# Row maxima and inverse row sums turned in one step, the inverses spread by DMA

## The chip, the cores and the metric

The kernel runs on one core of one Trainium2 chip. The metric is the device time of one execution in microseconds (us), lower is better. Its engines are named as in the profile: PE (TensorE), with its weight loads as PEld, DVE (VectorE), ACT (ScalarE), POOL (GpSimd) and SP (SyncE), which here only issues DMAs.

## The reference

One layer over 4 batches of 512 tokens, width 512: causal cross attention to a context of width 128 (16 query heads of width 32 in 4 groups that share a key and value head), then a feed-forward part with a router.

```python
q = _rms_norm(_layernorm(x), q_norm_w); k = _rms_norm(ctx, k_norm_w)     # heads of 32, then rope on both
scores = jnp.einsum('bgnqd,bgkd->bgnqk', qg, k) * scale
scores = jnp.where(causal, scores, -1e30)
attn = jax.nn.softmax(scores, axis=-1)
out = jnp.einsum('bgnqk,bgkd->bgnqd', attn, v)                           # v is ctx, unnormalised
x = x + out @ w_out.T
# then, on t = _layernorm(x): softmax router, top 4 of 128, 8 basis units silu(t Wg) * (t Wu)
# mixed by the chosen experts' normalised amplitudes, a down product, and a shared pair of units
x = x + mixed_down + shared_down
```

All is in float32. The large products split each operand into a high and a low part (fp32r) and add three products.

## The kernel before

**Units of work.** Attention is cut into 32 spans: u = (batch, half of the queries, key head), so a span is 4 heads of 256 query rows. `TH` is 2 (tiles of 128 rows in a half), `G` is 4 (heads of a span). A span of the first half sees 256 keys, one of the second half 512. `KV` is 4, and u below 4 (the first half of the first batch) goes another way than the rest.

**First pass.** For each of the 8 blocks (head, 128 rows) of a span PE makes scores (`pass_a`, L1408), DVE adds the mask and takes the row's negated maximum (`row_max`, L1130), ACT takes the exponential with the row sum as a by-product (`row_sum`, L891). DVE inverts the 8 sums per row (`inverse`, L1147).

**Second pass.** It needs scores with keys as rows. For u < 4 PE turns the exponentials of the first pass (`turn_probabilities`, L1419), and ACT copies them from PSUM to `pr` (L907). For u from 4 on PE makes the scores again, turned (`pass_b`, L1432), with the maxima as two more contraction rows of `q_st` (high and low part, rows 96 and 97), so that ACT's exponential (L909) needs no bias; POOL zeroes the diagonal blocks (L797). Then PE multiplies by the values (`value_products`, L1445) into `o_bank`, and DVE multiplies by the inverse row sums, turned and repeated for the 32 rows of each head (`attended`, L1156, reading `r_t`).

**Maxima.** DVE splits them (`maxima_split`, L1139, L1141, `mhl`, 8 columns), PE turns the 8 columns (`maxima_turn`, L1388, one pair of transposes), ACT copies to `m_t` (L883), and two DMAs on SP put the rows into `q_st` (L617).

**Inverses.** POOL repeats each of the 4 columns 32 times (`spread_inverse`, L787, `rrep`), PE turns the 128 columns (`inverse_turn`, L1397, a pair), ACT copies to `r_t` (L898).

**Queries and keys.** Normalised and roped tiles (`rope`, on DVE for tiles in `ROPE_DVE`, else on POOL) are turned by PE (L1367; the first four, three-fold, at L1380), split on ACT and DVE, and stacked by 12 DMAs on SP for each span's queries (L609) and for each half's keys (L599). Tiles 0 and 5 are keys of the first batch, 1 to 4 the queries of u0 to u3, 6 to 9 those of u4 to u7.

**Order.** Every engine runs through the same numbered slots (-40 to 247), and in each slot does what is due there, in an order of its own that its loop spells out. `span_slot(u)` is where a span starts; `CORE` and `LEAD` (u < 4) give the slot offsets of its steps, `SPAN` the lengths (7 and 6 slots in the first batch; after it 4 for the first half, 8 or 9 for the second). From slot 32 on, the products of the projection (L1513), of the feed-forward units (L1529) and of the down step (L1550) fill the slots, two tiles of 128 tokens at a time from the slots in `START`; `PAIR_AT` and `TILE_AT` give the offsets of the router's steps. Slot 32 begins at about 75 us, and a slot takes over 3 us from there. Weights come by DMA (L572), ACT makes their high half (L856), DVE (L1186) and POOL (L814, one chunk of four) the low half.

**Banks.** Short products (scores, turns, router) take three PSUM banks in turn, in the order of `short_products`; each waits until the reader of the product three before is done.

Of the kernel before, what the change touches and what calls it, by code (L numbers as in the profile page):

```python
# [35 lines left out]
PAIR_AT = dict(choose=9, keep=9, coefficients=9, turn_choice=10, mix=12)  # L36
# [23 lines left out]
def attention_and_mixture_kernel(nc, x, ctx_in, q_norm_w, k_norm_w, w_out, w_router, w_units, w_down,  # L60
# [48 lines left out]
    with common:  # L109
# [19 lines left out]
        mx, sums, rinv = (sb(n, [P, 2, TH, G]) for n in ("mx", "sums", "rinv"))  # L129
        mhl, m_t = sb("mhl", [P, 2, TH, 2 * G], F32R), sb("m_t", [2 * G, Q], F32R)  # L130
        rrep, r_t = sb("rrep", [P, TH, P]), sb("r_t", [P, Q])
# [45 lines left out]
        def sem(name):  # L177
# [10 lines left out]
        s_m = [sem(f"m{i}_landed") for i in range(2)]  # L188
        s_chunk = [[sem(f"chunk{i}_{h}_landed") for h in range(2)] for i in range(WR)]
# [17 lines left out]
            "pass_a", "row_max", "row_sum", "max_high", "max_low", "max_turned", "max_out"))  # L207
        s_rinv, s_rrep, s_rt1, s_rout = (sem(n) for n in (
            "row_inverse", "inverse_spread", "inverse_turned", "inverse_out"))
        s_pb, s_ex, s_sel, s_pv = (sem(n) for n in ("pass_b", "exp", "exp_masked", "value_product"))  # L210
# [231 lines left out]

        def query_tile(u):
            return u // KV * NB + u % KV + 1
# [14 lines left out]

        def probable(u, k):  # L460

            first = span(u)[1] * TH
            if u < KV or k < first:
                return s_ex, step_no(u, k) + 1
            return s_sel, (u - KV) * TH + k - first + 1
# [47 lines left out]
        def short_products(s):  # L513
# [5 lines left out]
            if (u := of_span(s, "inverse_turn")) is not None:  # L519
                found.append(("inverse", u))  # L520
            if (u := of_later_span(s, "maxima")) is not None:
                found.append(("maxima", u - KV))
            for n in tiles_in(s, "turn"):
                found += stacks(n)
            found += [("scores", u * G * TH + m) for u, m in first_pass_tiles(s)[1:]]
            if (p := routing(s, "turn_choice")) is not None:
                found.append(("choice", p))
            if (g := mixture(s, "turn_x")) is not None:
                found.append(("x", g))
            if (g := turned_down(s)) is not None:  # L530
                found += [("down", 2 * g), ("down", 2 * g + 1)]
            if (p := routing(s, "mix")) is not None:
                found.append(("mix", p))
            return found
# [4 lines left out]
        short_read = dict(maxima=s_mout, turn=s_tl, inverse=s_rout, scores=s_max, x=s_txl, route=s_lg,  # L539
# [37 lines left out]
        def sync_engine(e):  # L577
# [34 lines left out]
            def rows(u):  # L612
                e.wait_ge(s_mout, u - KV + 1)
                if u >= QR:
                    e.wait_ge(*second_pass_over(u - QR))
                for k in range(2):
                    e.dma_start(f32(q_st[MAXROW + k:MAXROW + k + 1, u % QR, :, :]),  # L617
                                f32(m_t[k * G:(k + 1) * G, :])).then_inc(s_m[u % 2], 16)
# [24 lines left out]
            for s in slots:  # L643
                for b in range(2, B):
                    if s == batch_slot(b) + CONTEXT:
                        load_ctx(b)
# [8 lines left out]
                if s == LOADS[0]:  # L655
                    load_ctx(1)
                    load_x(1)
                if s == LOADS[1]:
                    load_x(2)
                if s == LOADS[2]:  # L660
                    first_weights()
                if (u := of_later_span(s, "maxima")) is not None:
                    rows(u)
# [3 lines left out]
                if (u := queries_stacked_in(s)) is not None:  # L667
                    stack_queries(u)
# [5 lines left out]
        def pool_engine(e):  # L674
# [108 lines left out]
            def spread_inverse(u):  # L783
                e.wait_ge(s_rinv, u + 1)
                if u >= 1:
                    e.wait_ge(s_rt1, u)
                e.tensor_copy(heads(rrep[:]), rinv[:, u % 2].unsqueeze(3).broadcast_to([P, TH, G, D])  # L787
                              ).then_inc(s_rrep, 1)

            def mask_probabilities(u, k):  # L790
# [5 lines left out]
                e.wait_ge(s_ex, n + 1)  # L796
# [27 lines left out]
            for s in slots:  # L824
                if (u := of_span(s, "spread")) is not None:
                    spread_inverse(u)
                if (step := second_pass_step(s - SELECT)) is not None:
                    mask_probabilities(*step)
                if (hb := of_half(s, "query_scale")) is not None:
                    query_scale(hb)  # L830
                if (g := mixture(s, "scales")) is not None:
                    norm_scale(g)
                if (hb := of_half(s, "key_scale")) is not None:
                    key_scale(hb)
                if (u := attended_before(s)) is not None:
                    out_low(u)
                for i, k in splits(s, "low"):
                    if k in POOL_LOW:
                        weights_low(i, k)
                for n in tiles_in(s - 1, "rope"):  # L840
                    if not rope_on_dve(n):
                        rope_last(n)
# [10 lines left out]
        def scalar_engine(e):  # L853
# [25 lines left out]
            def maxima_out(u):  # L879
                e.wait_ge(s_mt, u - KV + 1)  # L880
                if u > KV:
                    e.wait_ge(*max_rows(u - 1))
                e.activation(m_t[:], short("maxima", u - KV)[0:2 * G, 0:Q], ACT.Copy).then_inc(s_mout, 1)  # L883
# [10 lines left out]
            def inverse_out(u):  # L894
                e.wait_ge(s_rt1, u + 1)
                if u >= 1:
                    e.wait_ge(s_att, u)
                e.activation(r_t[:], short("inverse", u)[:, 0:Q], ACT.Copy).then_inc(s_rout, 1)  # L898

            def exponential(u, k):  # L900
                n = step_no(u, k)
# [74 lines left out]
            for s in slots:  # L976
                if (u := of_span(s, "inverse_turn")) is not None:
                    inverse_out(u)
                if (u := of_later_span(s, "maxima")) is not None:
                    maxima_out(u)  # L980
                if (u := attended_before(s)) is not None:
                    out_high(u)
                for n in tiles_in(s, "turn"):
                    high(n)
                if s - 1 in fillers and fillers[s - 1][0] == "unit":
                    tanh(fillers[s - 1])
                if (g := mixture(s, "turn_x")) is not None:
                    x_high(g)
                if (p := routing(s, "choose")) is not None:
                    router_exp(p)  # L990
                if (g := mixture(s, "normalize")) is not None:
                    normalize(g)
                if (g := mixture(s, "route")) is not None:
# [677 lines left out]
```

## Time and profile before

| | us |
|---|---|
| median of 3 runs | 856.6 |
| lowest and highest run | 853.35, 859.44 |
| the profiled execution, device time | 855.69 |
| its span, first to last instruction | 853.9 |
| PE, DVE, ACT, POOL busy in it | 786.6, 668.9, 577.1, 520.9 |

In the profile a row of a group gives the line, the engine, the operation, the tiles it writes and reads, the count, the busy time, the mean of one in ns, and the idle time of the engine just before such instructions with what ended it. Matmuls overlap in the pipeline, so the mean of one is longer than what one adds; the distance between starts tells that. A row of the timeline gives start and length in us. SPq is SP's issue of a DMA; its length is the issue, not the transfer.

### The profile page before, as it was taken

The page shows a single profiled execution, that of the slowest core. Times are in us where ns is not written, and L with a number is a line of the kernel's source. Part 1 is how long each engine was busy: PE and PEld are TensorE (multiplying, and loading weights), DVE is VectorE, ACT ScalarE, POOL GpSimd, SP SyncE. Part 2 cuts the span into 40 slices and gives each one's busy share as a digit, 9 for nine tenths or more (in the row PEclk, how much of TensorE's full clock was granted, in tenths as well). Part 3 has the DMA queues.
Part 4 walks back from the last instruction along what each step waited for, and adds up shares of the span by engine and source line. Part 5 has one row for each costly group of instructions (what it writes and reads, how often), then busy time and mean ns, then how long its engine had stood idle before and what let it go on. Part 6 is the DMA issues. An engine that isn't in the chain of part 4 may idle for free. (4 is left out here: it accounts for less than half of the span.)

```text
span 853.9 us, 15213 instructions
## 1 busy us (share of the span) xinstructions
PE 786.6 (92%) x4180; PEld 609.4 (71%) x4180; DVE 668.9 (78%) x1635; ACT 577.1 (68%) x1413; POOL 520.9 (61%) x687
## 2 busy tenths in 40 slices
PE   2668789989999999989999999989999999999998
PEld 1546567767777777768777778767777777787876
DVE  6647777878988887878988897878878786687774
ACT  2668877767677676777777776677777775654542
POOL 4347547896378745897477843897466624661561
PEclk9977799999999999999999999999999999999999
DMA  8221234544454435644444445445444435453550
GB/s 298 87 52 37 83 95 147 186 139 128 148 195 163 141 129 196 222 153 134 148 155 166 148 150 178 148 155 169 148 162 162 154 112 161 160 186 122 200 196 25
DMA packets 57795, 126.76 MB, mean 148 GB/s; under 512 B 12048, under 2 KB 28784, under 8 KB 57712
## 3 DMA queue, kind: packets, MB, share of 16 engines
q1 hardware_dynamic: 57712, 125.78, 44.4%
q8 instruction: 36, 0.59, 0.3%
q14 instruction: 47, 0.39, 0.1%
HBM read 107.16 MB, written 4.19 MB: 130 GB/s over the span
## 5 line engine op out<-in xcount | busy, mean ns | idle before, releaser
L1529 PE MATMUL u<-w_h,t_h 128*128 128x512 f32 x640 | 260.1, 406 | 8.4 <-POOL w_l L814 5.6
L1529 PE MATMUL u<-w_l,t_h 128*128 128x512 f32 x640 | 251.2, 393 | 0.0
L1529 PE MATMUL u<-w_h,t_l 128*128 128x512 f32 x640 | 251.0, 392 | 0.0
L1186 DVE TENSOR_TENSOR w_l<-w_raw,w_h 128x512 fp32r<-128x512 f32 x288 | 249.2, 893 | 0.0
L856 ACT ACTIVATE w_h<-w_raw 128x512 fp32r<-128x512 f32 x384 | 219.2, 622 | 13.2 <-DMA w_raw<-in_w_units 13.0
L891 ACT ACTIVATE scores<-scores,mx 128x384 f32<-128x384 f32 (+1 forms) x224 | 128.5, 574 | 78.9 <-DVE mx L1130 77.4
L814 POOL TENSOR_TENSOR w_l<-w_raw,w_h 128x512 fp32r<-128x512 f32 x96 | 135.4, 1410 | 69.6 <-ACT w_h L856 69.1
L1529 PEld LDWEIGHTS u<-w_h,t_h 128*128 128x128 f32 x640 | 120.9, 189 | 37.6 <-POOL w_l L814 9.0
L822 POOL TENSOR_TENSOR macc<-macc,gb 128x256 f32<-128x256 f32 x112 | 105.8, 946 | 65.0 <-DVE gb L1287 64.7
L1130 DVE CUSTOM_DVE_ANT_0 scores<-s,mask_qk 128x384 f32<-128x384 f32 (+1 forms) x224 | 112.4, 504 | 37.7 <-PE s L1408 36.7
L1529 PEld LDWEIGHTS u<-w_h,t_l 128*128 128x128 f32 x640 | 120.5, 188 | 27.1
L1529 PEld LDWEIGHTS u<-w_l,t_h 128*128 128x128 f32 x640 | 121.3, 189 | 20.3
L1408 PE MATMUL s<-k_st,q_st 96*128 96x256 f32 (+2 forms) x256 | 92.1, 374 | 11.7 <-DVE q_st L1115 4.7
L1268 DVE SCALAR_TENSOR_TENSOR th<-th,u 128x256 f32<-128x256 f32 x160 | 66.6, 416 | 46.0 <-ACT th L956 45.2
L909 ACT ACTIVATE pr<-pair 128x1024 f32<-128x1024 f32 x88 | 77.7, 883 | 28.8 <-PE pair L1432 28.7
L956 ACT ACTIVATE th<-u 128x256 f32<-128x256 f32 x160 | 60.2, 376 | 46.0 <-PE u L1529 45.5
L780 POOL TENSOR_TENSOR o_l<-att,o_h 128x256 fp32r<-128x256 f32 x32 | 27.3, 853 | 78.5 <-ACT o_h L914 78.5
L1408 PEld LDWEIGHTS s<-k_st,q_st 96*128 96x128 f32 x256 | 51.5, 206 | 31.2 <-issue 16.7
L1287 DVE SCALAR_TENSOR_TENSOR gb<-th,wt,u 128x256 f32<-128x256 f32 x112 | 53.9, 481 | 16.4 <-DVE th L1268 0.5
L1432 PE MATMUL pair<-q_st,k_st 98*128 98x512 f32 x148 | 53.1, 426 | 1.2 <-ACT pr L909 1.2
L797 POOL TENSOR_SCALAR_AFFINE_SELECT pr<-pr 128x512 f32<-128x512 f32 x56 | 39.0, 697 | 23.8 <-ACT pr L909 23.6
L1445 PE MATMUL o_bank<-pr,ct 128*32 128x256 f32 (+1 forms) x768 | 46.5, 362 | 0.0
(146 smaller groups left out, 1206.7 us busy)
## 6 DMA issues: line engine op xcount, KB each, us to landing
w_raw<-in_w_units SPq DMA_DIRECT2D x160, 512.0 KB, 4.2
w_raw<-in_w_out_t SPq DMA_DIRECT2D x16, 512.0 KB, 4.2
w_raw<-in_shared_w_down SPq DMA_DIRECT2D x16, 512.0 KB, 4.5
q_st<-turned_h SPq DMA_DIRECT2D x232, 32.0 KB, 1.9
out<-x SPq DMA_DIRECT2D x16, 256.0 KB, 2.1
q_st<-turned_l SPq DMA_DIRECT2D x116, 32.0 KB, 1.9
x<-in_x SPq DMA_DIRECT2D x3, 1024.0 KB, 9.2
k_st<-turned_h SPq DMA_DIRECT2D x56, 32.0 KB, 1.9
```

Source lines behind the costliest of these rows:

```text
L814: e.tensor_tensor(w_l[:, i % WR, k, :], w_raw[:, i % WR, k, :], f32(w_h[:, i % WR, k, :]), ALU.subtract).then_inc(s_wlp, 1)
L822: e.tensor_tensor(total, total, gb[:, adds_before(w, g) % 2, :], ALU.add).then_inc(s_acc, 1)
L856: e.activation(w_h[:, i % WR, k, :], w_raw[:, i % WR, k, :], ACT.Copy).then_inc(s_wh, 1)
L891: e.activation(s, s, ACT.Exp, bias=mx[:, u % 2, t, j:j + 1], scale=-1.0, accum_out=sums[:, u % 2, t, j:j + 1]).then_inc(s_sum, 1)
L909: e.activation(pr[:, n % PR, 0:width], pair[:, 0:width], ACT.Exp, scale=-1.0).then_inc(s_ex, 1)
L956: e.activation(th[:, n % 2, :], u_bank[filler_no[f] % 2][:, 0:I], ACT.Tanh, scale=0.5).then_inc(s_tanh, 1)
L1130: e.tensor_tensor_reduce(masked_scores(u, m), short("scores", i)[:, 0:width], mask_qk[:, T - width:T], 1.0, 3e38, ALU.add, ALU.min, mx[:, ...
L1186: e.tensor_tensor(w_l[:, i % WR, k, :], w_raw[:, i % WR, k, :], f32(w_h[:, i % WR, k, :]), ALU.subtract).then_inc(s_wl, 1)
L1268: e.scalar_tensor_tensor(th[:, n % 2, :], th[:, n % 2, :], 1.0, up, ALU.add, ALU.mult).then_inc(s_ga, 1)
L1287: e.scalar_tensor_tensor(to, th[:, n % 2, :], scale, gate_v, ALU.mult, ALU.mult).then_inc(s_gb, 1)
L1408: e.matmul(short("scores", i)[:, 0:w], q_st[0:MAXROW, u % QR, j, t * P:(t + 1) * P], k_st[0:MAXROW, (b * KV + kv) % KR, 0:w], start=True, ...
L1529: last = e.matmul(u_bank[n % 2][:], t[:, k, cols], ww[:, i % WR, k, :], start=(k == 0 and m == 0), stop=(k == KC - 1 and m == 2))
```

## The change

- The spread on POOL, `rrep`, the inverse's own turn and its copy on ACT go.
- `maxima_turn` becomes `rows_turn`: for u from 4 on it turns 12 columns of one buffer `rhl` (4 inverses, 4 high and 4 low maxima) in one pair of transposes, for u < 4 the 4 inverses alone. It waits for the split and for the reciprocal. Its slot is the maxima's (0 of the span; 2 for u < 4), and on PE, as before among the turns, it now stands after the tile's turn.
- ACT copies the rows to one buffer `rhl_t` (`rows_out`), after the landing of the DMAs that read it for the span before.
- SP issues the two maxima rows as before and then one DMA per span that writes `r_t` (now two buffers, 128 x 256) from the 4 inverse rows, each repeated 32 times. `attended` waits for its landing.
- For u < 4, DVE copies the second of the two turned blocks of the second pass (512 columns) in ACT's place, and that second pass begins one slot earlier (4).
- The rope tiles on DVE are 0, 1, 3, 6 (before 0, 1, 2); several slots of the first tiles, keys, loads and moments move by one to three.
- The router's `choose` comes one slot earlier (8). Within the slots, each engine's list is put in another order: on PE the turn of x comes last of the short products, on DVE the inverse comes after `attended` and the moments, `choose` and `keep_largest` around the split, `coefficients` ahead of the weights' low halves; on SP the stacking of queries comes before the rows.

The diff, cut to its core:

```diff
-CORE = dict(split=-1, inverse=-1, maxima=0, spread=1, second_pass=3, inverse_turn=5,
+CORE = dict(split=-1, inverse=-1, maxima=0, second_pass=3,
             values=6, high=1)
-LEAD = dict(inverse=-1, spread=-1, second_pass=5, inverse_turn=5, values=9, high=0)
-FIRST_TILES = dict(rope=(-37, -34, -20, -12, -7, 5, 10, 17, 24, 30), turn=(-17, -15, -8, -1, 6, 13, 14, 21, 28, 34), stack=(4, 15, 22, 29, 35))
-ROPE_DVE = (0, 1, 2)
+LEAD = dict(inverse=0, maxima=2, second_pass=4, values=9, high=0)
+FIRST_TILES = dict(rope=(-36, -34, -20, -12, -7, 5, 10, 16, 24, 30), turn=(-17, -13, -8, -1, 6, 12, 14, 21, 27, 34), stack=(3, 15, 22, 29, 35))
+ROPE_DVE = (0, 1, 3, 6)
+COPY_DVE = (1,)
-PREP = dict(key_squares=(-39, 4, -29, -8), key_scale=(-37, 4, -28, -2), query_scale=(-35, 9, -23, 4), key_stack=(1, 15, -16, 8))
+PREP = dict(key_squares=(-39, 4, -29, -6), key_scale=(-37, 4, -29, -2), query_scale=(-35, 7, -23, 4), key_stack=(1, 15, -16, 8))
-ROPE3 = (-35, -33, -16, -11)
-LOADS, XLOAD, SELECT = (-12, 0, -5), 8, 1
+ROPE3 = (-35, -32, -17, -9)
+LOADS, XLOAD, SELECT = (-10, 0, -5), 8, 1
-PAIR_AT = dict(choose=9, keep=9, coefficients=9, turn_choice=10, mix=12)
+PAIR_AT = dict(choose=8, keep=9, coefficients=9, turn_choice=10, mix=12)
...
+        rhl, rhl_t = sb("rhl", [P, 2, TH, 3 * G]), sb("rhl_t", [3 * G, Q])
+        r_t = sb("r_t", [P, 2, Q])
...
             def rows(u):
-                e.wait_ge(s_mout, u - KV + 1)
-                if u >= QR:
+                e.wait_ge(s_mout, u + 1)
+                if u >= KV:
                     e.wait_ge(*second_pass_over(u - QR))
-                for k in range(2):
...
+                    for k in range(2):
+                        e.dma_start(f32(q_st[MAXROW + k:MAXROW + k + 1, u % QR, :, :]),
+                                    rhl_t[(k + 1) * G:(k + 2) * G, :]).then_inc(s_m[u % 2], 16)
+                if u >= 2:
+                    e.wait_ge(s_att, u - 1)
+                e.dma_start(r_t[:, u % 2, :], rhl_t[0:G, :].unsqueeze(1).broadcast_to([G, D, Q])
+                            ).then_inc(s_r[u % 2], 16)
...
-            def spread_inverse(u):
-                e.wait_ge(s_rinv, u + 1)
-                if u >= 1:
-                    e.wait_ge(s_rt1, u)
-                e.tensor_copy(heads(rrep[:]), rinv[:, u % 2].unsqueeze(3).broadcast_to([P, TH, G, D])
-                              ).then_inc(s_rrep, 1)
...
+            def rows_out(u):
+                n = 3 * G if u >= KV else G
+                e.wait_ge(s_mt, u + 1)
                 if u > KV:
                     e.wait_ge(*max_rows(u - 1))
+                if u >= 1:
+                    e.wait_ge(*inverse_rows(u - 1))
+                e.activation(rhl_t[0:n, :], short("rows", u)[0:n, 0:Q], ACT.Copy).then_inc(s_mout, 1)
...
+            def turned_copy(u, k):
+                n = step_no(u, k)
+                width = G * (Q - seen(u, k))
+                e.wait_ge(s_pb, n + 1)
+                if n >= PR:
+                    e.wait_ge(s_pv, n - PR + 1)
+                e.tensor_copy(pr[:, n % PR, 0:width], pair[:, 0:width]).then_inc(s_ex_v, 1)
...
+            def rows_turn(u):
+                n = 3 * G if u >= KV else G
+                if u >= KV:
+                    e.wait_ge(s_mlo, u - KV + 1)
+                e.wait_ge(s_rinv, u + 1)
+                e.wait_ge(*short_free("rows", u))
+                bank = short("rows", u)
                 for t in range(TH):
+                    last = e.transpose(bank[0:n, t * P:(t + 1) * P], rhl[:, u % 2, t, 0:n], ident[:])
                 last.then_inc(s_mt, 1)
-            def inverse_turn(u):
-                e.wait_ge(s_rrep, u + 1)
-                e.wait_ge(*short_free("inverse", u))
-                bank = short("inverse", u)
-                for t in range(TH):
-                    last = e.transpose(bank[:, t * P:(t + 1) * P], rrep[:, t, :], ident[:])
-                last.then_inc(s_rt1, 1)
```

## Rows read from the trace of the kernel before

**Rows 1.** Page, part 1: busy time, share of the span, instructions.

```profile
PE 786.6 (92%) x4180; PEld 609.4 (71%) x4180; DVE 668.9 (78%) x1635; ACT 577.1 (68%) x1413; POOL 520.9 (61%) x687
```

**Rows 2.** Busy time by stretch; then granted clock, DMA share, GB/s.

```profile
33.00:75.00 42.00, 31.90 (x170) 22.26 (x170) 24.53 (x105) 30.79 (x95) 22.83 (x46) 0.72 0.16 41
75.00:130.00 55.00, 45.49 (x250) 31.36 (x249) 42.09 (x116) 43.06 (x101) 31.66 (x50) 0.90 0.27 86
130.00:345.00 215.00, 209.30 (x1143) 163.26 (x1142) 179.44 (x439) 157.56 (x390) 148.07 (x193) 0.99 0.48 159
345.00:397.00 52.00, 47.47 (x268) 36.83 (x268) 42.69 (x113) 35.77 (x102) 47.85 (x67) 1.00 0.49 161
397.00:541.00 144.00, 141.79 (x769) 110.80 (x768) 122.31 (x290) 105.84 (x252) 87.47 (x111) 1.00 0.47 156
541.00:854.00 313.00, 299.49 (x1546) 236.75 (x1544) 237.26 (x521) 191.97 (x450) 171.40 (x194) 1.00 0.45 151
```

**Rows 3.** Waits of PE from 130 us on: total us, times, longest.

```profile
PE u L1529 <- POOL w_l L814: 5.6, 5, 1.9
PE s L1367 <- POOL r_b L774: 4.4, 4, 1.3
PE s L1388 <- DVE mhl L1141: 3.9, 10, 0.6
PE s L1474 <- DVE cf L1246: 3.6, 5, 1.4
```

**Rows 4.** Timeline of PE around one inverse's turn (start, length in us).

```profile
402.32 0.38 PE L1397 MATMUL s<-ident,rrep 128*128 128x128 f32 x2
...
402.77 0.40 PE L1529 MATMUL u<-w_l,t_h 128*128 128x512 f32 x1
403.00 0.40 PE L1529 MATMUL u<-w_h,t_l 128*128 128x512 f32 x1
```

**Rows 5.** Groups by line over the whole span.

```profile
L787 POOL COPY rrep<-rinv 128x256 f32<-128x256 f32 x32 | 19.6, 613 | 39.0 <-PE s L1397 29.2 <-DVE rinv L1147 9.7
...
L898 ACT ACTIVATE r_t<-s 128x256 f32<-128x256 f32 x32 | 12.0, 376 | 1.8 <-PE s L1397 1.6
...
L1035 DVE BATCH_NORM_STATS2 stats<-x 128x6 f32<-128x512 f32 x16 | 10.9, 679 | 0.0
...
L883 ACT ACTIVATE m_t<-s 8x256 fp32r<-8x256 f32 x28 | 10.3, 366 | 15.9 <-PE s L1388 15.7
```

**Rows 6.** Timeline of PE and DVE at two spans' maxima turns.

```profile
184.04 0.38 PE L1388 MATMUL s<-ident,mhl 128*8 128x128 f32 x2
...
184.69 0.20 DVE L1147 RECIPROCAL rinv<-sums 128x8 f32<-128x8 f32 x1 [0.81 <-ACT scores L891]
...
360.55 0.20 DVE L1147 RECIPROCAL rinv<-sums 128x8 f32<-128x8 f32 x1
...
360.59 0.38 PE L1388 MATMUL s<-ident,mhl 128*8 128x128 f32 x2 [0.61 <-DVE mhl L1141]
```

**Rows 7.** Timeline of SP, DVE and PE in the lead-in.

```profile
39.24 1.24 SPq L609 DMA_DIRECT2D q_st<-turned_h  x2
...
62.80 0.42 DVE L1156 TENSOR_TENSOR att<-o_bank,r_t 128x256 f32<-128x256 f32 x1
...
69.53 0.58 SPq L609 DMA_DIRECT2D q_st<-turned_l  x1
70.60 1.35 SPq L617 DMA_DIRECT2D q_st<-m_t  x2
...
74.67 0.89 PE L1432 MATMUL pair<-q_st,k_st 98*128 98x512 f32 x2
```

**Rows 8.** Page, part 6: KB of one DMA, median us to landing.

```profile
w_raw<-in_w_units SPq DMA_DIRECT2D x160, 512.0 KB, 4.2
...
q_st<-turned_l SPq DMA_DIRECT2D x116, 32.0 KB, 1.9
```

**Rows 9.** A wait of PE from 33 to 75 us.

```profile
PE s L1367 <- POOL r_b L774: 2.5, 1, 2.5
```

More of the change, by code:

```diff
@@ L188, in attention_and_mixture_kernel @@
         s_m = [sem(f"m{i}_landed") for i in range(2)]
+        s_r = [sem(f"inverse{i}_landed") for i in range(2)]
         s_chunk = [[sem(f"chunk{i}_{h}_landed") for h in range(2)] for i in range(WR)]
@@ L458, in last_span, with out_of_pair @@
             return c // KV * H * KV + KV + c % KV
+        copied_on_dve = lambda u, k: u < KV and k in COPY_DVE
+        def out_of_pair(u, k):
+            mine = copied_on_dve(u, k)
+            return (s_ex_v if mine else s_ex,
+                    sum(copied_on_dve(v, i) == mine for v in range(u + 1) for i in range(steps(v)) if (v, i) <= (u, k)))
         def probable(u, k):
@@ L518, in short_products @@
             found += [("scores", u * G * TH + m) for u, m in first_pass_tiles(s)[:1]]
[L519 to L522, printed above, removed]
             for n in tiles_in(s, "turn"):
                 found += stacks(n)
+            if (u := of_span(s, "maxima")) is not None:
+                found.append(("rows", u))
             found += [("scores", u * G * TH + m) for u, m in first_pass_tiles(s)[1:]]
@@ L537, in attention_and_mixture_kernel @@
         short_no = {f: i for i, f in enumerate(shorts)}
-        short_read = dict(maxima=s_mout, turn=s_tl, inverse=s_rout, scores=s_max, x=s_txl, route=s_lg,
+        short_read = dict(rows=s_mout, turn=s_tl, scores=s_max, x=s_txl, route=s_lg,
                           choice=s_cfo, mix=s_wt, down=s_dl)
@@ L654, in sync_engine @@
                         load_x(b)
[L655 to L662, printed above, removed]
+                if (u := queries_stacked_in(s)) is not None:
+                    stack_queries(u)
+                for b in range(2, B):
+                    if s == batch_slot(b) + CONTEXT:
+                        load_ctx(b)
+                if (u := of_span(s, "maxima")) is not None:
                     rows(u)
@@ L1315, in vector_engine @@
                     evict[fillers[s - 1][0]](fillers[s - 1])
-                for u, m in first_pass_tiles(s)[1:]:
-                    row_max(u, m)
-                if (p := routing(s, "choose")) is not None:
-                    choose(p)
-                if (g := mixture(s, "turn_x")) is not None:
-                    x_low(g)
-                if (p := routing(s, "keep")) is not None:
-                    keep_largest(p)
                 if s == START[0]:
@@ L1327, in vector_engine @@
                     resident_low()
-                if (g := turned_down(s)) is not None:
-                    for k in range(2):
-                        down_low(g, k)
+                for u, m in first_pass_tiles(s)[1:]:
+                    row_max(u, m)
+                if (p := routing(s, "keep")) is not None:
+                    keep_largest(p)
                 if (u := of_later_span(s, "split")) is not None:
                     maxima_split(u)
+                if (p := routing(s, "choose")) is not None:
+                    choose(p)
                 for n in tiles_in(s, "rope"):
@@ L1338, in vector_engine @@
                         rope_stacked(n)
+                if (g := mixture(s, "turn_x")) is not None:
+                    x_low(g)
+                if (g := turned_down(s)) is not None:
+                    for k in range(2):
+                        down_low(g, k)
                 if (g := mixture(s, "route")) is not None:
                     logits(g)
+                for g in moments_in(s):
+                    moments(g)
+                if (u := attended_in(s)) is not None:
+                    attended(u)
+                if (p := routing(s, "mix")) is not None:
+                    token_weights(p)
+                if (p := routing(s, "coefficients")) is not None:
+                    coefficients(p)
                 if (u := of_span(s, "inverse")) is not None:
                     inverse(u)
-                if (u := attended_in(s)) is not None:
-                    attended(u)
-                for g in moments_in(s):
-                    moments(g)
                 for i, k in splits(s, "low"):
@@ L1349, in vector_engine @@
                         weights_low(i, k)
-                if (p := routing(s, "coefficients")) is not None:
-                    coefficients(p)
-                if (p := routing(s, "mix")) is not None:
-                    token_weights(p)
+                if (step := second_pass_step(s)) is not None and copied_on_dve(*step):
+                    turned_copy(*step)
         def tensor_engine(e):
```

126 lines of the change are left out of this document (54 added, 72 removed).

## The prediction

> **What bounds the kernel.** I read the page first, then busy time by stretch, then the waits of PE, then single places in the timeline. By the page PE is busy for 92% of the span and no other engine for more than 78% [rows 1]. That is an average over unlike stages. The stretches show three. Before 130 us the span is a lead-in: from 33 to 75 us PE is busy for 31.9 of 42 us at a granted clock of 0.72, from 75 to 130 for 45.5 of 55 at 0.90. From 130 us on PE is busy for 698.1 of 724 us (the last four stretches), so there time is saved only by taking work from PE or by ending one of its 26 us of waits. One stretch differs: from 345 to 397 us PE idles for 4.5 us while POOL is busy for 47.9 of 52 [rows 2]. The waits of PE after 130 us are named in one table: POOL 10.0 us (the low halves of weights and the rope tiles), the maxima's split 3.9, the router's coefficients 3.6 [rows 3]. In the lead-in the chain of q and k stacking DMAs on SP sets the pace: they are issued without a gap from 39.24 us until about 70.1, and PE waits there for landings, for POOL's rope [rows 7, 9].
>
> **The change part by part.**
>
> *Turns.* Each of 28 spans (u from 4) had two pairs of transposes on PE, one for maxima, one for the spread inverses; now it has one pair of 12 columns. The first four keep one pair. A pair costs what it delays the next product: from 402.32 to 402.77 us, less the 0.23 us that a product of 512 columns takes anyway (402.77 to 403.00), 0.22 us [rows 4]. The new pair has as many moving columns, so I price it like the old. Saved: 28 x 0.22 = 6.2 us, on the bounding engine; the bounds are 5 and 7.
>
> *Copies.* ACT loses 28 evictions (60 before, 32 after, about 0.37 us each, 10 us), POOL 32 spreads of 0.61, 19.6 us [rows 5]. ACT isn't what PE waits for after 130 us, so its 10 us count as nothing; if ACT came to bind they would be a gain. POOL's do count where it is saturated. Three times in the run (once per later batch, in the four-slot spans; 345 to 397 us is the middle one) POOL works without a pause ahead of the waits that PE spends on it, and three spreads stand in each such run: 3 x 3 x 0.61 = 5.5 us. Taken: 5.0; bounds 0 (the next thing in POOL's queue is late too) and 10.0, all of PE's wait for POOL.
>
> *Router one slot earlier.* `choose` moves from 9 to 8, `coefficients` ahead of the weights' split on DVE. PE's turn of the choices waits 3.6 us for it in five places, at most 1.4 [rows 3]; a slot is over 3 us, so the wait goes: 3.6 saved. Bounds 2 and 5. ACT's exponential must follow the logits sooner, which costs DVE or ACT some tenths under PE's products.
>
> *The new wait.* PE's turn in slot 0 now needs the reciprocals as well, which need the last row sum of ACT. Behind it on PE stand the projection or unit products, everything. In two spans of before: the reciprocal ends at 184.89 where the maxima's turns began at 184.04, and at 360.75 against 360.59 [rows 6]. Over the 28 spans the reciprocal ends after the turns began in 17, by 3.6 us together, and 0.85 is the largest. Against this the tile's turn (one pair, 0.22 us) now stands ahead of the step and fills up to 0.22 in each of the 17, 3.7 us. In three spans the moments now stand ahead of the inverse on DVE: 0.68 of statistics [rows 5] and some 0.2 of aggregate, 2.6 us. Sum +2.5; bounds 0, and 28 x 0.85 = 24 if each became like the worst.
>
> *DMA and the lead-in.* An inverse now travels by a DMA of 128 KB. From u = 4 on it has well over 20 us between its issue (slot 0) and `attended` (slot 6 or 8), so only its 0.6 us on SP counts, hidden while SP waits for PE's last read of weights. The first four spans have no such cover. SP's chain of 12-DMA groups (u3, keys, u4, u5) begins at 39.24 because turned tile 4 comes then. The rope's new shares bring that forward: DVE drops tile 2 and takes 3 and 6, POOL takes 2. The first low half no longer stands behind tile 2's rope; I take 1.3 us. PE's 2.5 us wait for POOL's rope of tile 6 [rows 9] goes too, but what follows needs k and q landings of the full SP queue, so I count it as nothing. Against it, the transfers for u = 1, 2 and 3 stand in that chain behind the stacks. Two come before the end of u5's group: 69.53 + 0.59 - 1.3 + 2 x 0.63 = 70.1 us, where the transfer for u3 is issued. It lands after 1.9 us if it is like the 32 KB ones, at 72.0, and after 4.2 if like the 512 KB ones [rows 8]. ACT may not overwrite the one buffer before that, so the maxima of u4 leave ACT at 72.4 and SP takes them 1.8 us after 70.60. Their landing releases the second pass that began at 74.67 [rows 7]: near 75. ACT's queue stands still meanwhile, and likewise `attended` of u2, at 62.80 before, waits for a transfer issued near 62. Turning the first half a slot earlier hardly helps here; four DVE copies of 512 columns, about 0.7 us each, spare ACT as many and lie in DVE's idle time. Net for the lead-in: +1.5; bounds -3 (all 2.5 of the rope kept) and +6 (landing like 512 KB, and `attended` late by the same).
>
> The Trainium skill (DMA: Bandwidth & Descriptors, Rules for kernel authors) states that a DMA whose slowest dimension has fewer than 16 entries runs on no more engines than that; the source here has 4 outermost. By its rule each of four engines would carry 32 KB, as each of 16 does in a 512 KB load, so the 4.2 us landing would hold and the lead-in would cost 2.3 us more. No row of before shows this shape.
>
> *The rest* (a later turn of x on PE, other orders on ACT, DVE and SP) swaps work inside slots. ACT's copy of turned x may idle some tenths, hidden by PE's products. I count nothing; bounds -2 and +4.
>
> **Sum.** -6.2 - 5.0 - 3.6 + 2.5 + 1.5 = -10.8. The profiled span goes from 853.9 to 843.1; the device time of that execution was 1.8 above its span, so 844.9; the median of the three runs, 856.6, is 0.9 above that execution's 855.7, so 845.8.
>
> **The rivals.**
> 1. *The wait on row sums binds (slower).* Place: PE in slot 0 of each later span. Without the +2.5 the sum is -13.3; at W per span the result is -13.3 + 28 W. It ends slower than before from W = 0.48, and over 1% slower from 0.78. For it: row 184.69, where DVE idles 0.81 for ACT [rows 6]. Against it: ACT is free for a fifth of the steady stretches and loses 28 copies. At W = 1, 856.6 + 14.7 = 871.
> 2. *The lead-in gives it back.* The late inverses of u2 and u3 (and a clock that stays at its lower level, 1.2 GHz, longer for it) cost +6 to +8 instead of +1.5: about 851. For it: SP's unbroken chain. Against it: only two transfers are late, each by 2 to 4 us.
> 3. *POOL and clock both give more.* All 10 us of POOL's waits go, and the stretch of 75 to 130 us is granted 2.4 GHz throughout (at 0.90 about 11 us of it run at 1.2 GHz, worth up to 5): 845.8 - 5 - 4 = 837.
> 4. *Nothing from POOL or the orders.* PE's saved time turns up as waits for DVE, busy for 179 of 215 us [rows 2]: only the turns and router less the new costs, -5.8: 851.
>
> **How the numbers follow.** Forecast 0.47 (840 to 850 by itself), rival 1 0.12, rival 2 0.15, rival 3 0.12, rival 4 0.14. A measurement of this kernel can tell about 1% from no change, 8.6 us. Below 848.0 lie most of the forecast and rival 3: 0.57. Above 865.2 lies most of rival 1, and a tail of rival 2: 0.11. The rest is 0.32. The range of 835 to 860 leaves out most of rival 1 and a tail below rival 3.
>
> **What would show it.** After: PE has 56 fewer transposes, no wait on L1474's counterpart, and waits on POOL of about 5 us; the new turn's wait totals 4 to 9 us, named after DVE's reciprocal; the steady stretch from 130 us is about 12 us shorter. In the lead-in, DVE's `attended` for u2 or ACT's row copy for u4 waits for a DMA, and the second pass of u4 starts within 2 us of 75. I am wrong if the new turn waits for over 0.8 us in most spans, if PE's waits for POOL stay at 10 us, or if the second pass of u4 starts earlier than 72 or later than 79 us.

## The result: slower by 12.9%, and the profile after

| | before | after |
|---|---|---|
| median, us | 857.4 (4 runs, 853.35 to 859.44) | 967.6 (4 runs, 964.68 to 967.88) |
| ratio, 95% interval | | 1.129 [1.126, 1.132] |
| profiled span, us | 853.9 | 962.9 |
| PE busy, us | 786.6 | 816.4 |

The forecast of 845.8 and its range up to 860 are both missed, by over 100 us. The page of after, its parts 1, 4, 5 and 6; the 56 transposes are gone from PE:

```profile
PE 816.4 (85%) x4124; PEld 622.7 (65%) x4124; DVE 663.5 (69%) x1647; ACT 569.4 (59%) x1381; POOL 497.6 (52%) x647
...
PE 36%; SPq 29%; DMA 8%; ACT 6%; issue 5%; DVE 5%; POOL 2%; ACTq 0%; DVEq 0%; POOLq 0%
...
L1537 PE MATMUL u<-w_h,t_h 128*128 128x512 f32 x640 | 267.1, 417 | 41.5 <-DVE gb L1299 31.4
L864 ACT ACTIVATE w_h<-w_raw 128x512 fp32r<-128x512 f32 x384 | 219.2, 621 | 116.5 <-DMA w_raw<-in_w_units 86.0
...
w_raw<-in_w_units SPq DMA_DIRECT2D x160, 512.0 KB, 4.6
...
r_t<-rhl_t SPq DMA_DIRECT2D x32, 128.0 KB
```

Every engine is busy for a smaller share of the span [rows 1]. What is new is in the second row: the chain that ended last runs over SP's issues for 29% of the span. The same row of before names no issue of SP at all:

```profile
PE 25%; DVE 3%; POOL 2%; issue 1%; ACT 1%; DVEq 0%; POOLq 0%; ACTq 0%
```

The fourth row says who suffers: ACT, which splits the streamed weights, waits 86 us for their landing (13.0 in before). The landing itself takes 4.6 us from the issue, so the loads aren't slow; they are issued late. The timeline of SP shows why. First before, one four-slot span of the third batch:

```profile
346.59 1.29 SPq L617 DMA_DIRECT2D q_st<-m_t  x2
348.21 1.19 SPq L609 DMA_DIRECT2D q_st<-turned_h  x2
...
353.87 1.23 SPq L609 DMA_DIRECT2D q_st<-turned_h  x2
355.13 0.59 SPq L609 DMA_DIRECT2D q_st<-turned_l  x1
355.77 1.06 SPq L572 DMA_DIRECT2D w_raw<-in_w_units  x2
```

The same stretch of work in after:

```profile
368.50 1.31 SPq L629 DMA_DIRECT2D q_st<-rhl_t  x2
369.86 0.60 SPq L634 DMA_DIRECT2D r_t<-rhl_t  x1
370.50 0.47 SPq L639 DMA_DIRECT2D out<-x  x1
371.08 5.89 SPq L621 DMA_DIRECT2D q_st<-turned_h  x2
377.01 0.59 SPq L621 DMA_DIRECT2D q_st<-turned_l  x1
377.64 1.22 SPq L621 DMA_DIRECT2D q_st<-turned_h  x2
...
383.35 1.05 SPq L584 DMA_DIRECT2D w_raw<-in_w_units  x2
```

The inverse's DMA (L634) costs SP 0.60 us itself, and the issue right behind it (`out<-x`) is as short as ever. But the pair behind that takes 5.89 us where such a pair takes 1.22. In the spans without a store of `x`, which are most, the pair takes 5.1 us: 3.9 us more than it should. From the maxima rows to the next weight load it was 9.2 us and is now 14.9. The timeline of after, all engines, shows the load's lateness handed on, each row naming what ended the wait in front of it:

```profile
386.89 1.15 ACT L864 ACTIVATE w_h<-w_raw 128x512 fp32r<-128x512 f32 x2 [5.28 <-DMA w_raw<-in_w_units]
388.34 0.42 DVE L1280 SCALAR_TENSOR_TENSOR th<-th,u 128x256 f32<-128x256 f32 x1 [6.51 <-ACT th L963]
389.53 0.47 PE L1537 MATMUL u<-w_h,t_h 128*128 128x512 f32 x1 [4.69 <-DVE gb L1299]
...
390.08 0.63 PE L1537 MATMUL u<-w_h,t_l 128*128 128x512 f32 x1
...
390.51 0.63 PE L1537 MATMUL u<-w_h,t_h 128*128 128x512 f32 x1
...
390.93 0.63 PE L1537 MATMUL u<-w_l,t_h 128*128 128x512 f32 x1
```

ACT's tanh of the units (L963) stands behind the split on ACT, the gate on DVE behind the tanh, the next unit product on PE behind the gate. PE loses 4.69 us. The last three rows show a second loss. Behind the wait the products start 0.43 and 0.42 us apart, against 0.23 in [rows 4]: TensorE's clock has fallen to its lower level, 1.2 GHz, and the granted clock from 389 to 393 us is 0.63. Before this fall PE had stood idle. From the start of slot 52 to the end the granted clock is 0.96 in after and 1.00 in before, and PE is busy there for 704.3 us against 679.6, although it has 48 transposes less to do. So of the 84 us that this stretch is longer, some 25 are PE at work at the lower clock, and the rest is idle time.

Where the 109 us are, from the start of each slot on PE in both traces (after less before): 24.7 us by slot 52, the rest in the 22 spans from u8 to u29 (3.9 us each on the mean, 9.3 at most), and none behind them. The stretch from 130 to 854 us holds 636.17 us of PE's work in after, 698.05 in before.

The semaphore's updates from the inverse's DMA (the thirteenth of them): 12 of its 16 come 1.6 us behind the issue, at once, the other four singly at 7.3, 7.6, 7.8 and 8.0. So four engines carry it. The Trainium skill (DMA: Bandwidth & Descriptors, Why a DMA increments its semaphore by 16 and not by 1) states just this: only the engines in use post an update when their data is down, the issuing sequencer writes the rest at once, and the number of engines divides the slowest dimension, here 4. The trace agrees. Its 1 KB packets took some 149 ns each; those of a `q_st` stack, of the same size, 59 ns.

### The profile page after: what moved, and what is told of

It is laid out like the page before. It is cut to its first block, busy times and chain, and to the rows that moved or that the text cites. A ratio compares the mean times of both kernels' runs of the same rounds, so it can differ in the third digit from the quotient of the medians.

```text
span 962.9 us, 14992 instructions
## 1 busy us (share of the span) xinstructions
PE 816.4 (85%) x4124; PEld 622.7 (65%) x4124; DVE 663.5 (69%) x1647; ACT 569.4 (59%) x1381; POOL 497.6 (52%) x647
## 4 chain that ended last, share of the span: by engine, by line
PE 36%; SPq 29%; DMA 8%; ACT 6%; issue 5%; DVE 5%; POOL 2%; ACTq 0%; DVEq 0%; POOLq 0%
SPq L621 21%; PE u L1537 21%; PE u L1558 6%; DMA w_raw<-in_w_units 6%; SPq L611 3%; SPq L629 2%; ACT w_h L864 2%; DMA w_raw<-in_shared_w_down 2%; PE o_bank L1453 2%; PE pair L1440 2%; PE s L1416 1%; PE u L1521 1%; SPq L584 1%; DVE w_l L1198 1%; SPq L634 1%
## 5 line engine op out<-in xcount | busy, mean ns | idle before, releaser
L1537 PE MATMUL u<-w_h,t_h 128*128 128x512 f32 x640 | 267.1, 417 | 41.5 <-DVE gb L1299 31.4
L1537 PE MATMUL u<-w_l,t_h 128*128 128x512 f32 x640 | 256.3, 400 | 0.0
L1537 PE MATMUL u<-w_h,t_l 128*128 128x512 f32 x640 | 256.2, 400 | 0.0
L824 POOL TENSOR_TENSOR w_l<-w_raw,w_h 128x512 fp32r<-128x512 f32 x96 | 138.9, 1446 | 84.6 <-ACT w_h L864 83.7
L1537 PEld LDWEIGHTS u<-w_h,t_h 128*128 128x128 f32 x640 | 124.4, 194 | 78.0 <-issue 50.5
L832 POOL TENSOR_TENSOR macc<-macc,gb 128x256 f32<-128x256 f32 x112 | 101.7, 909 | 122.2 <-DVE gb L1299 122.0
L1537 PEld LDWEIGHTS u<-w_h,t_l 128*128 128x128 f32 x640 | 123.6, 193 | 28.5
L1537 PEld LDWEIGHTS u<-w_l,t_h 128*128 128x128 f32 x640 | 124.6, 195 | 20.5
L1416 PE MATMUL s<-k_st,q_st 96*128 96x256 f32 (+2 forms) x256 | 94.6, 384 | 30.5 <-ACT rhl_t L894 9.6
L963 ACT ACTIVATE th<-u 128x256 f32<-128x256 f32 x160 | 59.7, 373 | 47.3 <-PE u L1537 46.9
L1112 DVE TENSOR_TENSOR turned_l<-s,turned_h 128x256 fp32r<-128x256 f32 x36 | 15.2, 424 | 58.9 <-ACT turned_h L878 58.4
```

The source lines that it names most:

```text
L824: e.tensor_tensor(w_l[:, i % WR, k, :], w_raw[:, i % WR, k, :], f32(w_h[:, i % WR, k, :]), ALU.subtract).then_inc(s_wlp, 1)
L832: e.tensor_tensor(total, total, gb[:, adds_before(w, g) % 2, :], ALU.add).then_inc(s_acc, 1)
L1416: e.matmul(short("scores", i)[:, 0:w], q_st[0:MAXROW, u % QR, j, t * P:(t + 1) * P], k_st[0:MAXROW, (b * KV + kv) % KR, 0:w], start=True, ...
L1537: last = e.matmul(u_bank[n % 2][:], t[:, k, cols], ww[:, i % WR, k, :], start=(k == 0 and m == 0), stop=(k == KC - 1 and m == 2))
```

## The experiments

The theory, narrow DMA: a DMA from four rows, each read 32 times, occupies few engines for long, and SP's next issues stall behind it. Rivals: the landing of the inverses is late for `attended`; the turn waits for row sums (rival 1 of the prediction); the new orders are bad. Twelve kernels were timed, each against the kernel before.

**1. The DMA alone, added to before.** Idle DMAs into an unused tile, right behind the maxima rows of each span from u = 4 on:

```diff
+                e.dma_start(spare[:], mask_qk[0:G, 0:192].unsqueeze(1).broadcast_to([G, D, 192]))
```

> The kernel before, with one idle DMA per span from u4 on (28), issued by SP right behind the maxima rows: 4 source rows of 192 floats (constants of the mask), each repeated 32 times, into a spare tile that nobody reads. Nothing waits for it but its successor a span later. Theory T (the transfer itself: 4 outer rows run on few DMA engines, and SP's next issues stand behind it): 28 transfers of three quarters of the size, so 28/32 x 0.75 x 110 us = about 70 us slower, at least 40; issues of L609 behind it take about 2 to 3 us instead of 0.6. Rival S (the new wait for the reciprocals and the new orders of the slots cost the time): 28 x 0.6 us of issue on SP at most, so 857 to 870.

Measured: 916.2, ratio 1.069 [1.063, 1.074]. Nobody waits for this data, and yet it costs 59 us. Timeline of its SP: the DMA, then the next two issues at 4.10 us for a pair:

```profile
372.42 0.59 SPq L622 DMA_DIRECT2D spare<-mask_qk  x1
373.11 4.10 SPq L611 DMA_DIRECT2D q_st<-turned_h  x2
377.25 0.59 SPq L611 DMA_DIRECT2D q_st<-turned_l  x1
```

**2. The same bytes from 128 rows.**

```diff
+                e.dma_start(spare[:], mask_qk[:, 0:192])
```

> The kernel before with one idle DMA per span as in before_plus_one, of the same 128 packets and bytes, but from 128 source rows (192 floats each) instead of 4 repeated ones. Theory F (few DMA engines: the semaphore of the changed kernel's transfer gets 12 of its 16 at once and 4 one by one at 7 us): 860 to 870, only the issue's 0.6 us on SP is left. Rival, the bytes or the count of DMAs cost it: 916 like before_plus_one.

Measured: 858.0, 1.002 [1.000, 1.004]. Same count, size and place; only the source differs. It lands in 3.1 us, no issue behind it stalls. The shape of the DMA is the cause, not its presence.

**3. Four DMAs for one, so that 16 engines carry each.** In before (idle) and in after (real). Each reads one row 32 times, the repeats outermost:

```diff
+                for j in range(G):
+                    e.dma_start(spare[j * D:(j + 1) * D, :],
+                                mask_qk[j:j + 1, 0:192].unsqueeze(1).broadcast_to([1, D, 192]))
```

> The same idle bytes as in before_plus_one, but as four DMAs per span, one for each source row, so that the outermost dimension that is not 1 has 32 entries. Theory T: spread over more DMA engines, no stall in SP's issues: within 10 us of the kernel before, though SP issues 112 DMAs more. Rival S: the same as before_plus_one, 857 to 870. A third theory, that the bytes or the count of DMAs cost the time wherever they run: as slow as before_plus_one or slower.

> The changed kernel with its one inverse DMA per span as four, one per head, each repeating one row 32 times (32 entries outermost). Theory T: the 110 us go; 840 to 862, by what the first prediction got right of the rest (845.8) and 96 more issues of 0.6 us on SP, which in the saturated lead-in stand in the chain: about 855. Rival S: stays at 950 or more.

Measured: 897.9, 1.046 [1.042, 1.050], and 930.9, 1.084 [1.078, 1.090]. Better than one narrow DMA, but far from repaired. With 16 engines reading one partition the slower packets took 340 to 380 ns in the first kernel, 400 to 500 in the second, where four engines had taken 100 to 120 and 149. The data still comes sooner than by the one narrow DMA: a DMA lands after 3.2 and 4.0 us by the pages, the narrow ones after 6 and 7. SP doesn't stall, but issues 84 (96) DMAs more. The two causes are parted by:

**4. Four DMAs, each from 32 different rows.**

```diff
+                    e.dma_start(spare[j * D:(j + 1) * D, :], mask_qk[j * D:(j + 1) * D, 0:192])
```

> The kernel before with four idle DMAs per later span, each from 32 different rows of 768 bytes into 32 rows of the spare tile (112 DMAs as in the run of four narrow ones, 24 KB each). If the narrow source (one row read 32 times) made that run 40 us slower: 857 to 866, what 112 issues of 0.6 us cost where they aren't hidden. If the number of DMAs did it: near 898 again.

Measured: 889.5, 1.038 [1.034, 1.041]. The expectation from the narrow source fell: of the 40 us of the run with narrow ones only 8 are the source's (pages: the idle DMAs land in 3.2 us there, 2.2 here). The other 32 come with the number of DMAs. That it is SP's time in issuing them, and not the transfers, is read from the trace: a weight load lands 4.4 us behind its issue, as in before (4.2), and ACT waits for it all the same. The page and the waits of ACT, of the run with wide ones:

```profile
spare<-mask_qk SPq DMA_DIRECT2D x112, 24.0 KB, 2.2
...
ACT w_h L861 <- DMA w_raw<-in_w_units: 44.4, 28, 3.4
```

No transfer in this run is narrow or slow; 2.5 us more of plain issues in each span are enough to make the weights late (13.0 us of such waits in before). Summing the length of all SP issues from 75 us on, over the whole timeline of SP, puts the runs in one line:

| run | SP's issues, us | over before | time over before, us |
|---|---|---|---|
| before | 353 | | |
| plus one wide DMA | 373 | 19 | 1.5 |
| after, DMA cut to four rows (6) | 375 | 22 | 0 |
| mixed kernel without the router's edit (9) | 379 | 25 | 2 |
| after, 16 source rows (7) | 382 | 28 | 7 |
| plus four wide | 424 | 71 | 32 |
| plus four narrow | 428 | 74 | 40 |
| plus one narrow | 449 | 95 | 59 |
| after, four narrow | 451 | 98 | 72 |
| after, inverse from ACT's queue (5) | 484 | 131 | 89 |
| after | 488 | 135 | 110 |

Up to some 25 us (under 1 us a span) the added issues cost little; beyond that each added microsecond costs 0.7 to 1.0 in the end. These are sums over single profiled executions, so a difference of two or three microseconds between rows says nothing. The kernel before was near this bound. The busy figures don't show it, since issues aren't counted in them.

**5. The inverse's DMA from ACT's queue.**

```diff
+                e.dma_start(r_t[:, u % 2, :], rhl_t[0:G, :]...)        # in rows_out on ACT, not in rows on SP
```

> The changed kernel with the inverse DMA, unchanged in shape, issued from ACT's queue right behind ACT's copy of the rows instead of from SP's. If SP's stalled issues are what costs the time: 860 to 880. If the four DMA engines' occupation costs it, by holding up packets of weights and queries whoever issues: 930 or more. If ACT's queue stalls in turn, between the two.

Measured: 946.9, 1.105 [1.101, 1.108]. The other queue gives back 20 us only. Its timeline of SP, where one DMA is issued by ACT at 361.31:

```profile
361.31 3.96 SPq L629 DMA_DIRECT2D q_st<-rhl_t  x2
361.31 0.56 ACTq L893 DMA_DIRECT2D r_t<-rhl_t  x1
365.31 2.40 SPq L634 DMA_DIRECT2D out<-x  x1
```

SP's issues stall although the slow DMA isn't theirs. So what stalls them is shared by the two queues. Which part of the DMA path that is, the runs don't show.

**6. After with the DMA cut to its four rows.** The spread over the 32 rows of each head is left out (`r_t` is set to one at the start); all waits, turns and orders are those of after:

```diff
-                e.dma_start(r_t[:, u % 2, :], rhl_t[0:G, :].unsqueeze(1).broadcast_to([G, D, Q])
+                e.dma_start(r_t[0:G, u % 2, :], rhl_t[0:G, :]
```

> The changed kernel with the inverse DMA cut to the 4 source rows into 4 partitions (not spread over a head's 32 rows: the attention output is then scaled wrongly, r_t being set to 1 once at the start). All waits, orders and the DMA's place stay. Theory T: 838 to 855, and it bounds what any cheaper spread could reach. Rival S: stays at 950 or more.

Measured: 857.9, 1.000 [0.998, 1.002]. All 110 us hang on the spreading of this DMA. Rival 1 falls, and so do the orders as a cause of the loss. But none of the 10.8 us gained by the forecast appear.

**7. After with 16 source rows.** DVE writes each inverse four times, PE turns 24 columns, the DMA reads 16 rows 8 times each; the result is whole:

```diff
-                e.reciprocal(rhl[:, u % 2, :, 0:G], sums[:, u % 2])
+                e.reciprocal(rhl[:, u % 2, :, 0:4 * G].rearrange("p t (h c) -> p t h c", c=4),
+                             sums[:, u % 2].unsqueeze(3).broadcast_to([P, TH, G, 4]))
```

> The changed kernel with each inverse written four times by DVE's reciprocal, so that 16 inverse rows (and 8 of maxima) are turned, and the one DMA per span reads 16 rows, each repeated 8 times: same bytes, one issue, 16 entries outermost. Theory F: 855 to 868, near after_small (857.9). Rival, that repeating a source row is slow on any number of engines, or that the bytes cost it: 900 or more.

Measured: 863.1, 1.008 [1.005, 1.011]. It lands in 3.4 us, and the second issue behind it takes some 0.7 us in most spans instead of 0.6. That repairs some 103 of the 110 us. It is the remedy that the Trainium skill (DMA: Bandwidth & Descriptors, Rules for kernel authors) implies, an outermost dimension of 16; experiment 3, with 16 engines too but one source row, shows that this alone isn't enough.

**8. The two maxima DMAs of before as one.** Fewer issues than before:

> The kernel before with the two maxima DMAs of a span as one (8 rows into partitions 96 and 97), 28 issues of 0.65 us fewer on SP. If SP's issue time behind the rows reaches PE at any length (before_plus_four: 70 us more of issue cost 40): 846 to 853. If the kernel before just has slack enough there: the same, 857 to 860.

Measured: 855.7, 0.999 [0.997, 1.002]. The sum of SP's issues falls by 16 us and nothing is gained: before stands just on the free side of the bend.

**9. Before's lead-in, the merged turn only from u = 4 on** (16 source rows), and the same with the router's edit. The orders are those of before but for one, which the expectation doesn't name: on PE the rows' turn stands behind the tile's turn, as in after.

```diff
+                if u >= KV:
+                    e.reciprocal(...)                          # into rhl, four times; else as before
...
-PAIR_AT = dict(choose=9, keep=9, coefficients=9, turn_choice=10, mix=12)
+PAIR_AT = dict(choose=8, keep=9, coefficients=9, turn_choice=10, mix=12)
```

> The kernel before with its lead-in (u below 4) and all its orders unchanged; from u = 4 on one turn of 24 columns (16 inverse columns, each inverse four times, 8 maxima columns), one row copy on ACT and one inverse DMA from 16 rows, no spread on POOL and no turn and copy of the inverse. Theory (the steady terms of the prediction are right, and what ate them in the run with the small DMA was the other orders and the lead-in): -6.1 turns, -5.8 POOL, +1.9 wait on the turn, +1.3 DMA as between the runs of 16 and of 4 rows: about 849, ratio 0.990. Rival (what is taken from POOL's waits turns up in other waits whatever the orders): 854 to 858, ratio 0.997 to 1.001.

> The same with the router's choice one slot earlier and its coefficients ahead of the weights' low halves on DVE. Theory: the turn of the choices no longer waits, 3.5 us less than the run without it, about 845.5, ratio 0.986. Rival: DVE is so late elsewhere that the wait moves to the gate or the low halves, no difference to the run without it.

Measured: 859.6, 1.002 [1.000, 1.004], and 855.5, 0.997 [0.995, 0.999]. The rival held for the first: in this setting too the merged turn brings nothing. Why is read from its trace below. The router's edit held, 4.1 us between the two. This mixed kernel is the only one here that is faster than before beyond its interval, by 0.3%.

**10. The router's edit alone in before.**

> The kernel before with one part of the change alone: the router's choice one slot earlier (8) and its coefficients ahead of the weights' low halves on DVE. Theory (the router's term stands by itself, as it came out between the two mixed kernels, 4.1 us): PE's waits on the coefficients, 3.6 us in the kernel before, go, about 854, ratio 0.995 to 0.996. Rival (it pays only where the spreads are gone from POOL or the turn of the inverses from PE): 857 to 858, ratio 0.999 to 1.0.

Measured: 854.9, 0.9985 [0.9968, 1.0002]: 2 us less in the medians (against 856.75 on its chip), not separable from nothing.

## Why the prediction was wrong, step by step

**The failing step: what the inverse's DMA costs SP (DMA and the lead-in).** "From u = 4 on it has well over 20 us between its issue and `attended`, so only its 0.6 us on SP counts, hidden while SP waits for PE's last read of weights." The cover for the data was there: after the lead-in `attended` never waits for `r_t`. Its only two waits, in DVE's timeline of after:

```profile
55.31 0.42 DVE L1168 TENSOR_TENSOR att<-o_bank,r_t 128x256 f32<-128x256 f32 x1 [3.12 <-DMA r_t<-rhl_t]
75.11 0.42 DVE L1168 TENSOR_TENSOR att<-o_bank,r_t 128x256 f32<-128x256 f32 x1 [7.20 <-DMA r_t<-rhl_t]
```

(Leaving the lead-in, ACT's copy of the rows waited for one landing more, 3.9 us.) But the price on SP was not 0.6 us: it was 0.6 and 3.9 of stall behind it in most spans, 4.7 in the one shown. Over the execution SP's issues take 136 us more than in before, of which the 32 added ones are 19. And "hidden" was asserted, not summed over a span. In the span of before shown above SP pauses for 2.6 us, from 357.30 to 359.89. In the next two, the timeline of before shows none:

```profile
361.85 1.30 SPq L617 DMA_DIRECT2D q_st<-m_t  x2
363.25 1.19 SPq L609 DMA_DIRECT2D q_st<-turned_h  x2
...
371.16 1.05 SPq L572 DMA_DIRECT2D w_raw<-in_w_units  x2
372.31 0.51 SPq L599 DMA_DIRECT2D k_st<-turned_h  x1
...
379.84 1.05 SPq L572 DMA_DIRECT2D w_raw<-in_w_units  x2
380.99 1.30 SPq L617 DMA_DIRECT2D q_st<-m_t  x2
...
390.47 1.05 SPq L572 DMA_DIRECT2D w_raw<-in_shared_w_down  x2
397.52 0.81 SPq L572 DMA_DIRECT2D w_raw<-in_w_units  x2
```

From 361.85 to 391.52 SP issues without a pause of more than 0.15 us between the rows, two spans' queries, a half's keys and three pairs of weight loads. There is no room in those 30 us, and 6 us of it after them. The prediction called SP's chain the pace-maker of the lead-in and doesn't make the same reading for the later spans.

**The landing.** 1.9 us was taken, 4.2 kept as an upper bound, 7 to 8 is what it took. The bound failed on the price of a packet: each of the four engines moves 32 packets of 1 KB, and at 149 ns they alone fill 4.8 us. In the lead-in this helps to make `attended` of u2 start at 75.11 instead of 62.80, and the second pass of u4 at 91.19 instead of 74.67 [rows 7] (the mark of being wrong was 79). By slot 52 after is 24.7 us late, where +1.5 was forecast. Even with the cut DMA of experiment 6 the lead-in is 5.7 us longer and this second pass starts at 80.67. That is only in part the inverses' detour over a DMA. In experiment 6 `attended` of u0 and u1 are already 3.3 and 4.1 us later than in before, and wait there for PE's `o_bank`; for the landing DVE waits once, 1.6 us at u2. With the lead-in of before (the first kernel of experiment 9) slot 52 is 3.0 us late. So a part belongs to the lead-in's other edits, which no run takes apart. The clock stays low for longer too, as rival 2 says: from 75 to 130 us the granted clock was 0.90 in before [rows 2], 0.77 in experiment 6, 0.74 in after. Rival 2 (+6 to +8) had about the size that experiment 6 shows; for the real DMA it was three to four times too small.

**Turns (-6.2).** Right in sign, somewhat large. PE's busy time from the start of slot 52 to the end is 679.6 us in before, 676.2 in experiment 6, 677.3 in 7 and 674.6 in the first kernel of 9: 2.3 to 5.0 less, where the 24 turns of this stretch were priced at 5.3.

**Copies (POOL, -5.0).** Right for the wait it named: PE's wait for POOL's low halves, 5.6 and 0.7 us before [rows 3], is 0.4 in experiment 7 from 130 us on. In the first kernel of experiment 9 it is 3.6. Right also that POOL's rope wait might stay. All waits of PE on POOL together, 10.9 us in before, are 7.8 in experiment 7 and 10.0 in the first kernel of 9, not 5. The rows of PE's waits in experiment 7:

```profile
PE s L1382 <- POOL r_b L791: 5.4, 7, 1.3
PE s L1406 <- issue: 4.7, 6, 1.5
PE s L1406 <- DVE rhl L1145: 3.3, 5, 1.0
PE u L1538 <- DVE gb L1300: 2.8, 4, 1.2
...
PE o_bank L1454 <- POOL pr L807: 1.8, 2, 0.9
PE s L1506 <- DVE mx L1135: 1.2, 3, 0.6
...
PE u L1522 <- POOL w_l L824: 0.4, 2, 0.2
```

What was taken away came back under other names: waits for the gate, for POOL's masking, for the maxima at the turns ahead of the down step, none of which stood in [rows 3]. This is rival 4, "PE's saved time turns up as waits". It shows best in the first kernel of experiment 9, whose lead-in and orders are those of before but for the one named. Page, part 1:

```profile
span 858.3 us, 14988 instructions
...
PE 781.9 (91%) x4124; PEld 603.8 (70%) x4124; DVE 671.7 (78%) x1635; ACT 568.8 (66%) x1385; POOL 506.2 (59%) x659
```

PE is busy 4.7 us less than before [rows 1], and the span 4.4 longer: its idle time grew by 9. (These are two single executions; the medians are 1.7 us apart.) Its waits from 130 us on:

```profile
PE s L1386 <- POOL r_b L786: 6.2, 8, 1.7
PE s L1517 <- DVE turned_l L1120: 4.2, 3, 2.0
PE s L1494 <- DVE cf L1265: 3.7, 5, 1.4
PE u L1549 <- POOL w_l L826: 3.1, 3, 1.1
```

The second row is new: the turned tile's low half (L1120) comes late. The timeline of this kernel shows what it waited for, in one of the three places:

```profile
400.98 1.15 ACT L868 ACTIVATE w_h<-w_raw 128x512 fp32r<-128x512 f32 x2 [1.59 <-DMA w_raw<-in_shared_w_down]
...
402.69 0.42 DVE L1120 TENSOR_TENSOR turned_l<-s,turned_h 128x256 fp32r<-128x256 f32 x1 [1.81 <-ACT turned_h L882]
...
403.26 0.41 PE L1517 MATMUL s<-ident,macc 128*128 128x128 f32 x2 [1.29 <-DVE turned_l L1120]
```

It is SP again. ACT waits for a weight load that SP issues at 396.83, at the end of a stretch without a pause, and the tile's high half stands behind the split on ACT. (In before the split of this load, at 397.54, waits for nothing.) The other two places read the same. PE suffers from it because of the order of the turns: the product three before L1517 is now the tile's turn, where in before it was the maxima's. The page agrees, its part 4: SP's issues are 7% of the chain that ended last, in before none. So a part of what was saved went where the 110 us went, into weights issued late. This kernel with before's order of the turns and with the one maxima DMA of experiment 8 was not run; whether the merged turn then gains anything is open.

**Router (-3.6).** Right: the row of the coefficients (3.7 above, 3.6 in [rows 3]) is gone in every kernel with the edit, and 4.1 us are gained between the two kernels of experiment 9. Alone in before about 2 us are.

**The new wait (+2.5).** Right. From 130 us on PE waits 3.9 us at the old maxima turn; in experiment 6 it waits 6.7 at the new one (3.2 named after DVE's reciprocal, 3.5 with no releaser in the profile): +2.8. Rival 1 did not occur.

So without the DMA's stall the steady part would have been about level (from slot 52 to the end 705.6 us in before, 704.0 in experiment 6, 704.6 in 7), not 12 us shorter, and the lead-in longer: rivals 2 and 4 together. The forecast missed by 12 us in its terms for PE, POOL and the lead-in (experiment 6, 857.9 against 845.8), and by 110 in a term that it held to be nothing, the inverse's DMA in SP's queue.

## What to carry to other kernels

Cost a DMA three ways: its data's landing, its issue, and what it does to the issues behind it. Look in the issuing engine's timeline for stretches without a pause, as for any engine, since the busy figures leave it out. Don't repeat few rows many times in one DMA: replicate on an engine until the source has at least 16 rows, or leave the spread to an idle engine. A few microseconds taken from one of several engines that all run near their limit can return as a wait for the next; look for the wait that would be second, and count the queue of the weights' DMAs among those engines.

## What the runs showed of the hardware

- A 128 KB SBUF copy from 4 rows, each read 32 times, landed after 7.1 to 8.0 us, one from 16 rows after 3.4, and 96 KB from 128 different rows after 3.1 by the page.
- Sixteen engines reading one row at the same time took up to 340 to 500 ns for a packet, four engines with a row each 100 to 149.
- The first issue behind the narrow 128 KB DMA took its usual 0.6 us. The second and third took 3.8 and 1.3 in most spans, 2.7 to 3.3 and 2.6 to 3.0 behind a store of `x`. Behind the 96 KB one the second took 3.3 to 3.8 in most spans. When the DMA was issued from ACT's queue, SP's issues stalled too (3.3 and 2.4 us in the place shown).
- A plain issue of a stack on SP takes 0.59 us. 84 more DMAs than in the run with one wide DMA, of 24 KB each, cost 31 us in a kernel in whose chain that ended last no issue of SP stood.
- After 4.69 us without work PE's products started 0.43 us apart instead of 0.23, at a granted clock of 0.63 from 389 to 393 us.
